# Late shared-expert units and both sums regions added in PSUM, units taken out of the gathers' way, weights loaded one pair per tile

## What is computed

```python
x = _layernorm(x + _L0_attn_ref(x, ...))              # decayed linear attention, 32 heads of 64
# _L0_ffn_ref: E, K, F = 64 experts, 6 per token, 96 wide; CAP = 48 tokens per expert
topk_w, topk_ids = _grouped_topk(x @ gate_w, bias)
y = _routed_moe(x, topk_w, topk_ids, w_gate, w_up, w_down)   # gather rows, silu(gate)*up, down, segment_sum
shared = silu(x @ ws_gate) * (x @ ws_up) @ ws_down
out = _layernorm(x + (y + shared))
```

## Time and profile before

| | us |
|---|---|
| median of 3 runs | 1367.67 |
| the profiled execution, its own time | 1362.8 |
| its span | 1361.0 |
| attention and its tail, to the last mask of the router | 0 to 1198 |
| counts, search, indices, to the first gather | 1198 to 1216.6 |
| tiles, to the last scatter's issue | 1216.6 to 1306.6 |
| loads of `sums` issued, to the end | 1310.6 to 1361.0 |

### The profile page before, as it was taken

The page is one execution under the profiler, slowest core; times in us unless marked ns, Lnnn a source line. Parts: engine busy times, 40 slices in busy tenths (PEclk is TensorE's granted clock), DMA queues, the critical chain, the costliest instruction groups (busy, mean ns, idle before and its releaser), DMA issues.

```text
span 1361.0 us, 39593 instructions
## 1 busy us (share of the span) xinstructions
PE 1291.1 (95%) x15260; PEld 1102.1 (81%) x15260; DVE 1029.9 (76%) x2327; ACT 927.8 (68%) x1746; POOL 493.1 (36%) x422
## 2 busy tenths in 40 slices
PE   7999999999999999999999999999999999978970
PEld 5788888888888888888888888888888888865550
DVE  6677878787878787888878787888787888753227
ACT  7667777777777677777777777777777777533434
POOL 0224233424232333324233423242333423335756
PEclk9999999999999999999999999999999999979995
DMA  8700000001000000000000000000000016558665
GB/s 297 261 2 10 27 9 27 9 3 32 2 26 9 26 10 26 9 27 9 26 9 27 9 13 23 10 26 17 27 17 26 17 38 197 158 170 244 107 195 203
DMA packets 47198, 81.11 MB, mean 60 GB/s; under 512 B 4464, under 2 KB 29136, under 8 KB 46160
## 3 DMA queue, kind: packets, MB, share of 16 engines
q1 hardware_dynamic: 37968, 65.58, 14.5%
q0 software_dynamic: 4608, 7.08, 3.0%
q10 hardware_dynamic: 4480, 6.29, 1.3%
HBM read 56.26 MB, written 22.68 MB: 58 GB/s over the span
## 4 chain that ended last, share of the span: by engine, by line
PE 85%; DVE 5%; DMA 4%; issue 3%; ACT 2%; POOL 1%; ACTq 0%; SPq 0%; DVEq 0%; POOLq 0%
PE pA L558 25%; PE pB L558 24%; PE pO L657 12%; PE pC L643 10%; PE pS L620 10%; DMA sums<-sb_stage,sb_sidx 3%; PE pC L558 1%; PE pS L558 1%; DVE sb_W L1195 1%; DVE sb_nmr L1654 1%; PE pC L682 1%; ACT sb_W L1174 0%; DVE sb_W L1642 0%; ACT sb_W L898 0%; POOL sb_stage L1738 0%
## 5 line engine op out<-in xcount | busy, mean ns | idle before, releaser
L1684 POOL TENSOR_TENSOR sb_vl<-sb_v,sb_vh 128x512 f16<-128x512 f32 x121 | 153.9, 1272 | 680.4 <-ACT sb_vh L944 680.4
L558 PE MATMUL pB<-sb_xh,sb_W 128*128 128x256 f16 x2048 | 349.6, 273 | 0.0
L1246 DVE TENSOR_TENSOR sb_S<-pS,sb_D 128x1024 f32<-128x1024 f32 x248 | 236.0, 952 | 120.5 <-PE pS L620 120.5
L952 ACT ACTIVATE sb_Shl<-sb_S 128x1024 f16<-128x1024 f32 x242 | 204.3, 844 | 110.9 <-DVE sb_S L1246 109.6
L558 PE MATMUL pB<-sb_xl,sb_W 128*128 128x256 f16 x1024 | 279.3, 273 | 0.0
L1252 DVE TENSOR_TENSOR sb_Shl<-sb_S,sb_Shl 128x1536 f16<-128x1536 f32 x121 | 225.4, 1863 | 10.4 <-ACT sb_Shl L952 10.1
L558 PEld LDWEIGHTS pB<-sb_xh,sb_W 128*128 128x128 f16 x2048 | 200.2, 99 | 22.8 <-issue 0.4
L558 PE MATMUL pA<-sb_xh,sb_W 128*128 128x256 f16 x1024 | 175.8, 274 | 10.2 <-DVE sb_W L1195 5.6
L558 PE MATMUL pA<-sb_W,sb_xh 128*128 128x256 f16 x1024 | 177.0, 275 | 3.7 <-ACT sb_qh L919 3.7
L657 PE MATMUL pO<-sb_Wo,sb_yh 128*128 128x256 f16 x1016 | 173.3, 273 | 0.0
L958 ACT ACTIVATE sb_gt<-pB 128x512 f32<-128x512 f32 x128 | 76.4, 597 | 140.9 <-PE pB L558 140.9
(11 more groups left out here) (290 smaller groups left out, 2711.9 us busy)
## 6 DMA issues: line engine op xcount, KB each, us to landing
sb_stage<-wprep SPq DMA_DIRECT2D x7, 1280.0 KB, 7.0
sb_W<-sums SPq DMA_DIRECT2D x16, 512.0 KB, 10.5
sb_W<-w_experts SPq DMA_DIRECT2D x17, 384.0 KB, 3.8
gather_rows<-sb_xr SPq DMA_DIRECT2D x16, 320.0 KB, 2.4
sb_xs<-xT SPq DMA_DIRECT2D x16, 256.0 KB, 2.9
sb_D<-decay SPq DMA_DIRECT2D x8, 512.0 KB, 7.9
sb_xn<-x SPq DMA_DIRECT2D x16, 256.0 KB, 3.0
sums<-sb_xr SPq DMA_DIRECT2D x16, 256.0 KB, 2.2
```

Source lines behind the costliest of these rows:

```text
L558: last = nc.tensor.matmul(dst, a, m, start=(i == 0), stop=(i == len(terms) - 1), **kw)
L952: nc.scalar.activation(Sh[:, :, a:z_], S[:, :, a:z_], ACT.Copy).then_inc(s_Sh, 1)
L1246: nc.vector.tensor_tensor(scores_at(h)[:, :, a:z_], pS[:, :, a:z_], d[:, :, 0:z_ - a], ALU.mult).then_inc(s_Sm, 1)
L1684: nc.gpsimd.tensor_tensor(vl[q % 2][:, :, :], v32[:, :, :], vh[q % 2][:, :, :], ALU.subtract).then_inc(s_vl, 1)
```

## The change

Five edits, all behind the attention.

1. **Late units in PSUM.** `unit_keep` and GpSimd's add (L1768) are gone. `late_down(j)` leaves unit 8 + i in a PSUM bank of its own (`pLate`), with the accumulation left open; `add_sums(c)` lets TensorE add both regions of chunk c to it, by multiplying them with the identity. VectorE's statistics and ScalarE's last step read chunks 8 to 15 from PSUM, and VectorE's add stays for chunks 0 to 7 alone. ScalarE does all late `unit_inner` ahead of the finals.
2. **Products.** The products of units 7 to 11 (`BY_DVE`) move from GpSimd to VectorE; GpSimd's two memsets go ahead of its waits on the norm.
3. **Order on TensorE and ScalarE.** `count` ahead of `unit_down(3)`, `running_counts` ahead of `unit_inner(4)`, `unit_gate_up(7)` ahead of the first `spread_ids`; `last_low_x1` ahead of the first `spread_equals` on VectorE. Each `spread_ids(n)` and `spread_equals(n)` from the third on is one tile later.
4. **Scatter ahead of gather**, for a tile; the transposed rows move into `x1T`, and `OUTBUF` is 6.
5. **Weights.** A pair p waits for tile p - 18 done, no longer for groups of three tiles that release four pairs at once.

```diff
-OUTBUF = 4
+OUTBUF = 6
...
+        pLateGU = [pA, pO]
+        pLate = [pB, pC] + [pS[:, i, :] for i in range(4)] + [pA, pO]
...
+        BY_DVE = range(UNITS_AHEAD - 1, UNITS_AHEAD + 4)
...
             for p in range(RING, PAIRS):
-                sp.wait_ge(s_md, KINDS * ((p - RING) // 4 + 1))
+                sp.wait_ge(s_md, max(KINDS * ((p - RING) // 4 + 1), p - 18))
                 load_pair(p)
...
+            def late_down(j):
+
+                pe.wait_ge(*shared_product(j))
+                pe.wait_ge(s_uact, j + 1)
+                for k in range(FIN):
+                    last = nc.tensor.matmul(pLate[j - UNITS_AHEAD][:, k * HID:(k + 1) * HID], us[0:FF, j % 2, k:T:FIN], wsd[:, :],
+                                            start=(k == 0), stop=False, skip_group_check=True)
+                last.then_inc(s_udn, 1)
+
+            def add_sums(c):
+
+                pe.wait_ge(s_fl[c], 16)
+                for k in range(FIN):
+                    for r in range(REGIONS):
+                        last = nc.tensor.matmul(pLate[c - UNITS_AHEAD][:, k * HID:(k + 1) * HID], ident[:, :], fin[c][:, r, k, :],
+                                                start=False, stop=(r == REGIONS - 1), skip_group_check=True)
+                last.then_inc(s_fp, 1)
...
-            unit_inner(UNITS_AHEAD)
-            for j in range(UNITS_AHEAD, UNITS_AHEAD + 4):
-                unit_inner(j + 1)
-                unit_keep(j)
+            for j in range(UNITS_AHEAD, SEQS):
+                unit_inner(j)
             for c in range(FINALS):
                 act.wait_ge(s_nm, c + 1)
                 for k in range(FIN):
-                    last = nc.scalar.activation(fin[c][:, 1, k, :], fin[c][:, 0, k, :], ACT.Identity,
+                    last = nc.scalar.activation(fin[c][:, 1, k, :], whole_rows(c, k), ACT.Identity,
...
-            for j in range(1, UNITS_AHEAD):
+            for j in range(1, UNITS_AHEAD - 1):
                 unit_product(j)
...
             for p in range(TILES):
+                scatter(p)
                 if p + AHEAD < TILES:
                     gather(p + AHEAD)
-                scatter(p)
-
-            for j in range(UNITS_AHEAD, UNITS_AHEAD + 5):
-                unit_product(j)
+
+            unit_product(UNITS_AHEAD + 4)
+            unit_product(UNITS_AHEAD + 5)
             for c in range(FINALS + 2):
-                if UNITS_AHEAD <= c < FINALS:
-                    pool.wait_ge(s_fl[c], 16)
-                    pool.wait_ge(s_uev, c + 1)
-                    nc.gpsimd.tensor_tensor(fin[c][:, 1, :, :], fin[c][:, 1, :, :], late_sh[c - UNITS_AHEAD], ALU.add).then_inc(s_fp, 1)
```

More of the change, by code:

```diff
@@ L257, in block_kernel @@
         wo = carve(P, OUTBUF, HID)
-        xgT = carve(P, 2, NC * P)
-        xgT = [xgT[:, 0, :], xgT[:, 1, :]] + [v32[:, t, :] for t in range(NT)]
+        xgT = [x1T[:, t, :] for t in range(NC)] + [v32[:, t, :] for t in range(NT)]
         xgT = [a.rearrange("p (c n) -> p c n", c=NC) for a in xgT]
@@ L391, in block_kernel, with shared_product @@
         HALVES = [(0, T), (T, T + P)]
+        BY_DVE = range(UNITS_AHEAD - 1, UNITS_AHEAD + 4)
+        def shared_product(j):
+            if j in BY_DVE:
+                return s_usd, j - BY_DVE.start + 1
+            return s_ush, len([i for i in range(j + 1) if i not in BY_DVE])
         def has(g):
@@ L410, in whole, with whole_rows @@
             return isinstance(h, int) and (h < WHOLE or h == LAST)
+        def whole_rows(c, k):
+            if c >= UNITS_AHEAD:
+                return pLate[c - UNITS_AHEAD][:, k * HID:(k + 1) * HID]
+            return fin[c][:, 0, k, :]
         def scores_at(h):
@@ L874, in _ @@
                     merge(p - 1)
+            pe.wait_ge(s_xgT, TILES)
             pe.wait_ge(s_mh, TILES)
+            pe.wait_ge(s_eq, TILES)
             pe.wait_ge(s_wo, TILES)
@@ L882, in _ @@
                     unit_gate_up(j + 1)
-                unit_down(j)
+                late_down(j)
+            for c in range(UNITS_AHEAD, FINALS):
+                add_sums(c)
         @block.scalar
@@ L1122, in evacuate @@
                 act.wait_ge(s_mT, t + 1)
+                if t == 0:
+                    act.wait_ge(s_x1l, SEQS)
                 wait(act, s_mgu, t + 1 - KINDS)
@@ L1611, in spread_equals @@
                 place_rows(n)
-            for n in range(3):
-                spread_equals(n)
             last_low_x1()
+            spread_equals(0)
+            unit_product(UNITS_AHEAD - 1)
+            spread_equals(1)
             def evacuate(t):
@@ L1632, in _ @@
                     evacuate(p - 1)
-                if p + 3 < TILES // EQB:
-                    spread_equals(p + 3)
+                if p + 2 < TILES // EQB:
+                    spread_equals(p + 2)
+            for j in range(UNITS_AHEAD, UNITS_AHEAD + 4):
+                unit_product(j)
             for c in range(FINALS + 2):
-                if c < FINALS:
+                if c < UNITS_AHEAD:
                     dve.wait_ge(s_fl[c], 16)
-                    if c >= UNITS_AHEAD:
-                        dve.wait_ge(s_fp, c - UNITS_AHEAD + 1)
                     nc.vector.tensor_tensor(fin[c][:, 0, :, :], fin[c][:, 0, :, :], fin[c][:, 1, :, :], ALU.add).then_inc(s_fadd, 1)
@@ L1659, in _ @@
                 if c < FINALS:
-                    dve.wait_ge(s_fadd, c + 1)
+                    if c < UNITS_AHEAD:
+                        dve.wait_ge(s_fadd, c + 1)
+                    else:
+                        dve.wait_ge(s_fp, c - UNITS_AHEAD + 1)
                     for k in range(FIN):
-                        last = nc.vector.bn_stats(st6[:, c % 2, k, :], fin[c][:, 0, k, :])
+                        last = nc.vector.bn_stats(st6[:, c % 2, k, :], whole_rows(c, k))
                     last.then_inc(s_fst, 1)
```

52 lines of the change are left out of this document (19 added, 33 removed).

## The result

The changed kernel takes 1350.47 us (median of 4 runs, 1349.62 to 1351.97), the kernel before 1366.74 (4 runs) beside it; the ratio is 0.9875, its 95% interval 0.9845 to 0.9904. That is 16.3 us faster, 9.0 us above my 1341.5: above the 1334 to 1347 that I gave my own forecast, inside the stated range of 1334 to 1353. The profiled execution took 1350.01, its span is 1348.1 (before: 1362.8 and 1361.0).

A forecast was written before the change was run, and what follows sets the result against it. Behind the unchanged, TensorE-bound attention, it took the hand-over, GpSimd's pace with slow scatter landings, and the finals as limits. Gains of 6.5 + 7.8 + 11.9 = 26.2 us from 1367.67 gave 1341.5, range 1334 to 1353 (own forecast 1334 to 1347).

The forecast's parts named there:

- a. Start: Hand-over from indices to first tiles: earlier counts, gathers and unit 7 gain 6.5 us (5 to 7).
- b. Weights one by one: Tiles: one weight pair per tile lets scatters land faster, losing 2.5 us instead of 10.3; gain 7.8 (0 to 10.3).
- GpSimd is the pace: Tiles: a gather with its gap and a scatter on GpSimd together take 3.19 us and set the pace.
- Past scatter 15 the 18.9 us stay: Last eight scatters, without gathers: the wait for landings sets their pace, 18.9 us, unchanged.
- the slow scatters: Rival, tiles, also called "The scatters stay slow": weights still slow the landings, term b is 0, time 1349.3; chance 0.15.
- the late start: Rival, hand-over: TensorE's spreads and unit 7 end as late as before, term a 0.5, time 1347.5; chance 0.05.
- the half clock: Rival, finals: TensorE's adds stay at clock 0.50, 3.5 us each, term c is 1, time 1352.4; chance 0.12.
- c. Finals: From the sums' loads to the end: without GpSimd's add the tail falls from 50.4 to 38.5 us; gain 11.9 (8 to 14).
- The other side: Rival, scatters 3 to 13: single loads keep every landing at 11 us, 5.9 a tile, time 1368.8; chance 0.06.

The follow-up runs named there:

- u_order: Changed kernel with the gather ahead of the scatter again: 1336.53 us, ratio 0.981; a second time on another chip 1338.83 us, ratio 0.9835.
- m_start: Changed kernel with the old hand-over order (counts behind a unit, three spreads ahead of the tiles, unit 7's product on GpSimd): 1357.99 us, ratio 0.9948.
- chip C: Group of runs on one chip, both kernels unchanged: the changed kernel 1350.72 us (0.9889), the kernel before 1365.66 us (1.0001).
- u_weights: Changed kernel with the old weight schedule, four pairs per three tiles: 1345.28 us, ratio 0.9866.
- chip A: Group of four runs on one chip, each undoing parts of the changed kernel: 1336.53, 1337.80, 1337.30 and 1345.28 us; the kernel before 1362.88.
- D: Group on another chip: changed kernel with scatters 0 to 11 only, 1331.51 us, and u_order a second time, 1338.83; the kernel before 1362.18.
- b_weights: Kernel before with one edit alone, one pair of weights per tile instead of four per three tiles: 1372.19 us, ratio 1.0041.
- m_finals: Changed kernel with the old finals (units evacuated by `unit_keep`, GpSimd's add, VectorE's add for all chunks): 1361.14 us, ratio 0.9966.
- again: The changed kernel itself, unchanged, a second time on another chip: 1350.93 us, ratio 0.9884.
- B: Group on one chip: again 1350.93 us, m_start 1357.99, m_finals 1361.14, b_weights 1372.19.

## Why the prediction was right, and where not

The traces side by side, us (starts of scatters from the timelines; "tail" is from the loads' issue to the end):

| | before, prompt | before, late (C) | u_order, prompt (A) | change, late (first) | change, late (C) |
|---|---|---|---|---|---|
| scatter 0 | 1228.69 | 1231.54 | 1220.40 | 1223.72 | 1224.19 |
| scatters 3 to 15 | 48.6 | 45.2 | 40.9 | 45.2 | 45.6 |
| scatters 15 to 23 | 18.9 | 18.5 | 18.2 | 24.9 | 25.5 |
| loads' issue | 1310.56 | 1310.82 | 1293.67 | 1308.33 | 1309.73 |
| tail | 50.4 | 49.4 | 40.5 | 39.8 | 40.5 |

*a. Start, 6.5.* Right way, and its size depends on the chip: scatter 0 is 4.9 us earlier by m_start (7.1 by the medians) and 7.4 between both kernels on chip C, but 8.3 in u_order against the trace of before, over my bound of 7. First gather 1207.74 for 1207.3; the first tile at 1213.30, 1.5 earlier than my 1214.8: TensorE's clock did not fall before it (granted clock 1.00 in 1208 to 1213, in this trace and in u_order's), which is 0.6 of it by my own 1214.2 for full clock; the rest is not traced. On a late chip that margin is lost again: ScalarE sees the first tile's product at 1217.95, 2.3 us behind its end.

*b. Weights one by one, 7.8.* This is the step that failed in the result, and not by its size but by its ground: "GpSimd is the pace", with 3.19 us a tile, and "Past scatter 15 the 18.9 us stay" hold where results are prompt. There the term measured 7.5 to 8.8 (u_weights), and my 2.5 us of remaining loss is u_order's 40.9 - 38.3 = 2.6 on chip A, 5.4 on D (0.25 x 11 is 2.75, not 2.5; it changes nothing). The landings came out too: where a scatter of u_order waited for one among the weights (4, 9 and 11), it started 6.9 to 7.6 us behind the last but one, against 4.4 to 4.6 behind the weights, where a landing takes some 3.8; that puts them at an estimated 6.1 to 6.9, for my 6.1. On a late chip the weights alone cost 6.1 in the kernel before (b_weights; in the changed kernel they were never undone there), and the start and the weights together, 14.3 forecast, move the loads by 1.1 us (both kernels on chip C). The table shows where it goes: between scatters 15 and 23. In the kernel before on chip C TensorE works ahead into the buffers while scatters wait for their landings (scatter 12 starts 7.6 us behind its copy), and the last eight follow at the landings' pace until that lead is used up (1.2 us at scatter 23). The change takes the landings' waits away, and then TensorE, which needs 3.1 to 3.8 us a tile when its results are late, is what every scatter waits for: in the first trace all 24 start 1.2 to 1.3 us behind their copies. Nothing of this was in my rivals, and that the result lies in the stated range is luck: the space above 1347 was made for the slow scatters, the late start and the half clock, and none of the three is what took the time. "The scatters stay slow" has the right size (1349.3) by the wrong mechanism, since no scatter of the first trace waited for a landing (14 times VectorE's copy ended its idling, 10 times nothing that the profile shows).

*c. Finals, 11.9.* Right mechanism, 1 to 2 us too high: 10.2 measured (m_finals), tail 39.8 for 38.5. The last load landed 31.5 us behind the issue (my 30 to 31), 8.3 followed (my 8), VectorE's shift takes 0.13 to 0.16 us, ScalarE goes in steps of 1.4 to 1.7. The half clock of the rival did come, at 3.78 us an add for my 3.5, but it did not stay: after chunks 8 and 9 the clock was back at 1.00, and TensorE had caught up before the last load landed. It cost nothing that shows: in the run again, where the adds followed the last unit without a pause, the clock was 1.00 through all of them (1.89 us for the first), and its end is 40.4 us behind the issue against 39.8. So the rival is out by its condition, that the clock stays low. The Trainium skill, "VectorE: DVE Perf Modes", section on the TRN2 errata, would have made each statistic from PSUM 65 ns longer by the prediction's estimate; here two take 0.76 us from PSUM and 0.74 from SBUF, and ScalarE's two scalings 1.02 from PSUM against 1.09, so counting nothing was right.

*The sum.* 26.2 forecast. By the spans on chip A it comes out as 26.8 (u_order, 1334.2 against 1361.0), but of other parts: 8.3 at scatter 0, 7.7 in scatters 3 to 15, 0.7 behind them, 9.9 in the tail and 0.2 between. Term a was 1.8 too small and term c 2.0 too large, and that the two cancel is luck. On the prompt chips the variants that each undo one small part gain 26.4, 25.1 and 25.6 (A) and 23.4 (D) against the kernel before; on late ones the change gains 15.2 (B), 14.8 (C) and 16.3 (first). The result's trace is a late one, set against a forecast from a prompt one. The change in whole was never timed on a prompt chip; its tiles 0 to 11 were, and they agree with the variants. *The other side*, scatters at 11 us for single loads, was wrong: at 5.9 us a tile twelve tiles would take 71 us, and they took 40.9 to 45.9 with single loads. The Trainium skill, "DMA: Bandwidth & Descriptors", section on queues, rings and completion order, has each DMA engine go round between the queues it has work for. The price that I drew from this rule, that one pair in flight holds the landings up as four do, is not borne out: u_order's are at 6.1 to 6.9 (estimate above) against 11.05.

What stays open is why results are late. For it being GpSimd's DMA instructions: all eleven scaled copies of the first trace that come 0.67 us or more late start within 0.3 us of a scatter's end, and none of the six prompt ones does; in the first tile ScalarE goes on 0.03 us ahead of the end of the last gather (1217.95 against 1217.04 + 0.94), in the kernel before on chip C 0.11 behind it (1225.44 against 1225.33) and VectorE beside it at 1225.41; and the lags of 1.5 us are gone from tile 18 on, when the last gather is out. Against: results are also passed on in the middle of a gather or scatter now and then (1278.22, VectorE's copy, 0.03 us behind its merge), and on chips A and D the same instructions hold nothing back. This is argued, not shown; so is why some chips do it.

## What to carry to other kernels

Ask of a trace whether the interval between an operation's end and its consumer's start is the same in every tile; if not, run the same program on another chip before a cause is sought in the program: here the extra 0.2 to 1.6 us came and went with the chip, and the worth of an edit can change sign with it (the weights: 7.5 gained in the changed kernel on a prompt chip, 6.1 lost in the kernel before on a late one). Before explaining the gap between a forecast and a result by the edits, profile both unchanged kernels on one chip: the two traces that I compared first were of a prompt and of a late one. And when a wait is taken away, price the engine that was working ahead behind it at its worst pace, not at its best.

## What the runs showed of the hardware

Two groups of runs on two chips differed from two others in more than speed. On A and D the kernel before took 1362.9 and 1362.2, on B and C 1366.1 and 1365.5, a quarter of a percent; the change took 1350.5 to 1350.9 on late chips, its close variants 1336.5 to 1338.8 on prompt ones. On B and C, and in the first trace of the change, matmul results reach ScalarE late while GpSimd issues indirect DMAs: up to 1.7 us at the scaled copies, 2.3 once in the first tile of the first trace (1217.95 against 1214.18 + 1.51), and 3.2 once on chip C (1225.44, where the transposes before it end at 1222.20). SyncE is held too (in the first trace its loads at 1265.99 started together with the scaled copy), and VectorE (1225.41 on chip C). On A and D all scaled copies came 0.05 to 0.08 us behind.

TensorE's granted clock was 0.50 for some 6 us after an idle stretch of 1.59 us in the finals of the first trace, and 1.00 in those of again; ScalarE's two scalings of a chunk take 1.02 us from PSUM and 1.09 from SBUF, VectorE's two statistics 0.76 and 0.74.
